# An attention and expert kernel on one core: context statistics spread over 64 tiles, the expert number read a tile ahead, spare rows filled whole, one weight matrix a batch

## The reference

```python
x = x + _L0_xattn(_layernorm(x), ctx, Wq, Wkv, Wo)          # 16 heads of 8, keys from ctx
x = x + _L0_ffn(_layernorm(x), ...)                          # 8 experts, the best one a token, 128->512->128, relu
x = x + _L1_xattn(_layernorm(x), ctx, ...)                   # two attentions of 16 heads of 32: on x (masked), then on ctx
x = x + _L1_ffn(_layernorm(x), ...)                          # 64 experts, the best four a token

def _L0_ffn_ref(x, Wr, br, W1, b1, W2, b2):
    expert_idx = jnp.argmax(xf @ Wr.T + br, axis=-1)
    h = jax.nn.relu(jnp.einsum('td,efd->etf', xf, W1) + b1[:, None, :])
    y = jnp.einsum('etf,edf->etd', h, W2) + b2[:, None, :]
    return y[expert_idx, jnp.arange(xf.shape[0])]

# in the second attention of _L1_xattn the context is normalised first:
yn = _ln(ctx, lny_g, lny_b)      # (ctx - mean) * (var + eps)^-0.5 * g + b
```

## Time and profile before

| | us |
|---|---|
| median of 3 runs | 2547.68 (2545.48 to 2555.09) |
| the profiled execution | 2546.86 |
| its span | 2545.1 |
| TensorE busy | 2252.1 (88%) |
| VectorE busy | 1950.9 (77%) |
| ScalarE busy | 1633.4 (64%) |
| GpSimd busy | 1534.1 (60%) |

### The profile page before, as it was taken

One profiled execution on the slowest core, in us unless ns is written; L12 is line 12 of the kernel. 1 busy time (PEld: TensorE's weight loads), 2 busy tenths in 40 slices (PEclk: granted clock), 3 DMA queues, 4 the chain that ended last, 5 costly groups with the idle time before them and its releaser, 6 DMA issues. The chain is left out here.

```text
span 2545.1 us, 87868 instructions
## 1 busy us (share of the span) xinstructions
PE 2252.1 (88%) x31528; PEld 1772.2 (70%) x31528; DVE 1950.9 (77%) x6038; ACT 1633.4 (64%) x3410; POOL 1534.1 (60%) x2510
## 2 busy tenths in 40 slices
PE   6999899958878999999999999999999999984755
PEld 5777677737876777777777777777777777763543
DVE  4778788756665788888888888888888888864558
ACT  4656566524544778888787787778788777763210
POOL 1555455543543577777677776776767777654456
PEclk9999999979988999999999999999999999995675
DMA  6333432112210011000000000000000000001247
GB/s 146 94 72 78 61 80 74 44 31 59 55 36 6 5 49 62 32 11 10 8 8 7 7 5 7 6 6 6 6 6 5 6 7 5 4 2 25 59 134 240
DMA packets 147867, 99.61 MB, mean 39 GB/s; under 512 B 47690, under 2 KB 129646, under 8 KB 147054
## 3 DMA queue, kind: packets, MB, share of 16 engines
q1 hardware_dynamic: 130798, 78.24, 12.4%
q0 software_dynamic: 16640, 15.76, 2.1%
HBM read 51.59 MB, written 56.80 MB: 43 GB/s over the span
## 5 line engine op out<-in xcount | busy, mean ns | idle before, releaser
L1267 POOL DMA_INDIRECT xs_d<-xpay,dest x256 | 267.4, 1045 | 138.5 <-issue 133.7
L1688 DVE TENSOR_REDUCE rdx<-core 128x16 f32<-128x1920 f32 (+1 forms) x128 | 282.8, 2209 | 54.3 <-PE core L806 54.2
L1169 POOL TENSOR_SCALAR st_h<-st_h 128x1 f32<-128x1 f32 x192 | 43.9, 229 | 354.7 <-DVE st_h L1366 354.5
L1107 ACT ACTIVATE kbd<-core 128x1024 f32<-128x1024 f32 (+1 forms) x256 | 245.8, 1011 | 8.4 <-PE core L844 8.4
L839 PE MATMUL core<-qT,pTm 32*128 32x128 f32 (+1 forms) x4096 | 194.9, 306 | 0.4 <-ACT nm3T L1093 0.4
L806 PEld LDWEIGHTS core<-pTm,qT 32*128 32x128 f32 x4096 | 125.9, 186 | 97.8 <-ACT qT L1111 93.2
L877 PE MATMUL bank<-li,shared 128*128 128x128 f32 x1024 | 147.2, 288 | 34.6 <-ACT shared L1129 34.4
L839 PEld LDWEIGHTS core<-qT,pTm 32*128 32x128 f32 (+1 forms) x4096 | 162.1, 186 | 19.2 <-issue 10.5
L1129 ACT ACT_TABLE_LOAD x128 | 164.2, 1283 | 2.2
L792 PE MATMUL bank<-yT,wk 128*128 128x128 f32 (+1 forms) x1024 | 146.4, 285 | 19.4 <-DVE denT L1627 17.1
L877 PEld LDWEIGHTS bank<-li,shared 128*128 128x128 f32 x1024 | 125.6, 193 | 50.4 <-ACT shared L1129 46.3
(11 more groups left out here) (243 smaller groups left out, 6986.0 us busy)
## 6 DMA issues: line engine op xcount, KB each, us to landing
c_d<-zeros SPq DMA_DIRECT2D x64, 256.0 KB
big<-c_d SPq DMA_DIRECT2D x64, 256.0 KB
big<-in_w SPq DMA_DIRECT2D x3, 2048.0 KB, 8.7
qT<-xs_d SPq DMA_DIRECT2D x72, 64.0 KB
vS<-xs_d SPq DMA_DIRECT2D x64, 65.0 KB, 1.9
xs_d<-zeros SPq DMA_DIRECT2D x8, 512.0 KB
yb<-y_d SPq DMA_DIRECT2D x64, 64.0 KB, 1.8
xs_d<-xpay,dest POOLq DMA_INDIRECT x256, 2.2
```

The lines of the kernel that those rows point to most:

```text
L1107: af(pTb[0:u.T, 2 * k:2 * k + 2, :], core[0:u.T, 2 * k:2 * k + 2, :], ACT.Exp, scale=SCALE).then_inc(s_pexp, 1)
L1267: g_.indirect_dma_start(out=xs1_d, out_offset=bass.IndirectOffsetOnAxis(ap=dest[:, v.bs, k:k + 1], axis=0), in_=xpay[:, v.bs, k, :], in_of ...
L1688: v_.tensor_reduce(nm_part[0], core[:, :, 0:4 * T].rearrange("p g (c t) -> p g c t", c=4), AX.X, ALU.max, negate=True)
```

## The change

- SyncE's order in the attention stage: one matrix a batch at batches 6 to 19, vectors at 20 and 22, eight fills at successive batches 24 to 31, the experts' weights two batches earlier. A fill now writes whole rows of 130 words from `pad_row` (128 zeros and the payload of an empty row), and `start_pads1` is gone.
- The zeroing of the tails (`zero_tail`) is done by SyncE for experts 0 to 3 and by ScalarE for 4 to 7.
- `context_stats` takes one batch a tile on tiles 0 to 63; `context_roots` takes eight batches at a time, after the scatters of tiles 7, 15, ..., 63; the rows are normalised on GpSimd for even batches (`context_even`, from tile 8 on) and on VectorE for odd ones (`context_odd`, from tile 13 on).
- VectorE loads the expert number of tile j+1 right behind `hidden0` of tile j.
- New waits: TensorE for GpSimd's last row (`s_cp`), VectorE for the fills before it uses their source again.

The diff, without the declarations and a few lines that only rename:

```diff
@@ -148,6 +148,7 @@
         ssa = woT0
         ssb = zeros
         xp = sb("xp", [P, 2, P])
+        pad_row = xp.rearrange("p u d -> p (u d)")[:, 0:P + 2]
         z3 = sb("z3", [P, P])
         z3T = sb("z3T", [P, P])
         xnS = sb("xnS", [P, 2, P])
@@ -391,6 +393,13 @@
             for j in range(n):
                 step(j // RING, j % RING, j < n - 1)
             after(n // RING - 1)
+
+        def zero_tail(eng, e):
+
+            at = eng.value_load(filled_i[0:1, e:e + 1], min_val=0, max_val=E0 * REGION0)
+            n = 9 if e == E0 - 1 else 1
+            eng.dma_start(xs_d[bass.ds(at, n * P), :].rearrange("(p a) d -> p a d", a=n),
+                          zeros[:, :].unsqueeze(1).to_broadcast([P, n, P])).then_inc(s_pad, 16)
 
         def earlier(i, k, d):
 
@@ -424,11 +433,14 @@
                 sp.dma_start(xres[:, FIRST:NB, :], x_v[:, FIRST:NB, :]).then_inc(s_x[1], 16)
                 sp.dma_start(ctx_sb[:, FIRST:NB, :], c_v[:, FIRST:NB, :]).then_inc(s_x[1], 16)
 
-            def load_matrices(a):
-                for n, dst in (("wq", wq), ("wk", wk), ("wv", wv), ("li1", li1), ("li2", li2),
-                               ("li3", li3), ("b2c", b2c)):
-                    rows = LAT if (a == 1 and n in ("wk", "wv")) else P
-                    sp.dma_start(dst[a][0:rows, :], t[f"{n}{a}"]).then_inc(s_load, 16)
+            matrices = [(n, dst, a) for a in range(2)
+                        for n, dst in (("wq", wq), ("wk", wk), ("wv", wv), ("li1", li1), ("li2", li2),
+                                       ("li3", li3), ("b2c", b2c))]
+
+            def load_matrix(k):
+                n, dst, a = matrices[k]
+                rows = LAT if (a == 1 and n in ("wk", "wv")) else P
+                sp.dma_start(dst[a][0:rows, :], t[f"{n}{a}"]).then_inc(s_load, 16)
 
             def load_vectors(a):
                 for n, dst in (("li1b", li1b), ("li3b", li3b), ("g_ln", g_ln), ("b_ln", b_ln)):
@@ -451,14 +463,10 @@
 
             def start_rows1(k):
 
-                e = slice(8 * k, 8 * k + 8)
-                sp.dma_start(xs1_v[:, e, 0:P], zeros[:, :].unsqueeze(1).to_broadcast([P, 8, P]))\
+                if k == 0:
+                    sp.wait_ge(s_made, 3)
+                sp.dma_start(xs1_v[:, 8 * k:8 * k + 8, :], pad_row.unsqueeze(1).to_broadcast([P, 8, P + 2]))\
                     .then_inc(s_init1, 16)
-
-            def start_pads1():
-
-                sp.dma_start(xs1_v[:, :, P:P + 2],
-                             padlist1[:, :].bitcast(F32).rearrange("p (e c) -> p e c", c=2)).then_inc(s_init1, 16)
 
             def load_experts0(k):
 
@@ -485,26 +493,21 @@
                     sp.nop(nofuse=True)
                 if u:
                     sp.dma_start(c_rows[u.batch], zeros4).then_inc(s_c0, 16)
-                if u and u.batch in (10, 14):
-                    load_matrices((u.batch - 10) // 4)
-                if u and u.batch in (12, 16):
-                    load_vectors((u.batch - 12) // 4)
-                if u and 18 <= u.batch < 34 and u.batch % 2 == 0:
-                    start_rows1((u.batch - 18) // 2)
-                if u and u.batch == 34:
-                    start_pads1()
-                if u and 36 <= u.batch <= 52 and u.batch % 2 == 0:
-                    load_experts0((u.batch - 36) // 2)
+                if u and 6 <= u.batch < 20:
+                    load_matrix(u.batch - 6)
+                if u and u.batch in (20, 22):
+                    load_vectors((u.batch - 20) // 2)
+                if u and 24 <= u.batch < 32:
+                    start_rows1(u.batch - 24)
+                if u and 34 <= u.batch <= 50 and u.batch % 2 == 0:
+                    load_experts0((u.batch - 34) // 2)
 
             pipeline_a(sp, half_a)
 
 
             sp.wait_ge(s_filled, 1)
-            for e in range(E0):
-                at = sp.value_load(filled_i[0:1, e:e + 1], min_val=0, max_val=E0 * REGION0)
-                n = 9 if e == E0 - 1 else 1
-                sp.dma_start(xs_d[bass.ds(at, n * P), :].rearrange("(p a) d -> p a d", a=n),
-                             zeros[:, :].unsqueeze(1).to_broadcast([P, n, P])).then_inc(s_pad, 16)
+            for e in range(E0 // 2):
+                zero_tail(sp, e)
             for s in range(2):
                 sp.wait_ge(s_sc[s], 32 * (NB // 2))
             sp.wait_ge(s_map, 1)
@@ -866,6 +869,7 @@
                 if h:
                     if h.a:
                         pe.wait_ge(s_c, 1)
+                        pe.wait_ge(s_cp, 1)
                     pe.wait_ge(s_z, h.n(1, 1))
                     last = tr(m0[:, 0:P], zS[:, :], ident)
                     if h.a:
@@ -1059,6 +1063,9 @@
                 if i * RING + k + 2 < TILES0:
                     weights0(i * RING + k + 2)
 
+            act.wait_ge(s_filled, 1)
+            for e in range(E0 // 2, E0):
+                zero_tail(act, e)
             act.wait_ge(s_map, 1)
             act.wait_ge(s_ffnw, 288)
             weights0(0)
@@ -1221,29 +1228,42 @@
                     bounds_check=dst.shape[0] - 1, oob_is_err=False)\
                     .then_inc(s_ysc[k], 16)
 
-            def context_roots():
-
-                pool.wait_ge(s_cvar, 1)
+            def context_roots(k):
+
+                eight = slice(8 * k, 8 * k + 8)
+                pool.wait_ge(s_cvar, k + 1)
                 pool.nop(nofuse=True)
-                g_.tensor_scalar(crs[:, :], cstat[:, :, 1], 1.0, EPS, ALU.mult, ALU.add).then_inc(s_cadd, 1)
-                pool.wait_ge(s_cadd, 1)
+                g_.tensor_scalar(crs[:, eight], cstat[:, eight, 1], 1.0, EPS, ALU.mult, ALU.add)\
+                    .then_inc(s_cadd, 1)
+                pool.wait_ge(s_cadd, k + 1)
                 pool.nop(nofuse=True)
-                g_.tensor_tensor(crs[:, :], crs[:, :], neghalf[0:CTX, :].to_broadcast([CTX, NB]), ALU.pow)\
+                g_.tensor_tensor(crs[:, eight], crs[:, eight], neghalf[0:CTX, :].to_broadcast([CTX, 8]), ALU.pow)\
                     .then_inc(s_crstd, 1)
+
+            def context_even(b):
+
+                pool.wait_ge(s_crstd, b // 8 + 1)
+                pool.nop(nofuse=True)
+                made = g_.tensor_scalar(ctx_sb[:, b, :], ctx_sb[:, b, :], cstat[:, b, 0:1], crs[:, b:b + 1],
+                                        ALU.subtract, ALU.mult)
+                if b == NB - 2:
+                    made.then_inc(s_cp, 1)
 
             def ids_there(j):
                 pool.wait_ge(s_ids[j % RING], j // RING * 32 + 32)
 
             tile_rows = lambda j: ids[:, j:j + 1]
             for j in range(TILES0):
-                if j == NB // 2 + 4:
-                    context_roots()
                 ids_there(j)
                 scatter(Unit(0, 0, RING, j), j % RING, y0_d, tile_rows(j), yS)
+                if j < NB and j % 8 == 7:
+                    context_roots(j // 8)
+                elif j >= 8 and j % 2 == 0:
+                    context_even(j - 8)
 
 
             pool.wait_ge(s_c0, 16 * (CROWS // (4 * P)))
-            pool.wait_ge(s_init1, 16 * 9)
+            pool.wait_ge(s_init1, 16 * 8)
 
 
             def mask_pair(u, k):
@@ -1373,11 +1393,13 @@
             v_.memset(onesb[:, :], 1.0)
             v_.memset(count1[:, :], 0.0)
             v_.memset(nma, 0.0)
+            v_.memset(pad_row[:, 0:P], 0.0)
             v_.memset(v_all[:, :], 0.0).then_inc(s_made, 1)
             dve.wait_ge(s_const, 80)
             copy(count0[:, :], slot0)
             copy(pickb[:, :, :], rS[:, :].rearrange("p (c t) -> p c t", c=4))
             copy(identb[:, :], ident)
+            copy(pad_row.bitcast(I32)[:, P:P + 2], padlist1[:, 0:2])
             copy(ltri[:, :], xx[:, :]).then_inc(s_made, 1)
             for s in range(2):
                 copy(pay_i[:, s, :, 0], cst_i[:, 258 + 4 * s:262 + 4 * s])
@@ -1514,6 +1536,7 @@
 
 
             dve.wait_ge(s_load, 16 * N_LOADS)
+            dve.wait_ge(s_init1, 16 * 8)
             for a in range(2):
                 v_.tensor_tensor(li3b[a][:, :], li3b[a][:, :], li1b[a][:, :], ALU.subtract)
 
@@ -1547,49 +1570,50 @@
 
             def context_stats(b):
 
-                six = (st_c, st_x) if b % 4 else (st_3, st_h)
-                for k in range(2):
-                    v_.bn_stats(six[k][0:CTX, 0:6], ctx_sb[:, b + k, :])
+                six = (st_c, st_x)[b % 2]
+                v_.bn_stats(six[0:CTX, 0:6], ctx_sb[:, b, :])
                 after()
-                for k in range(2):
-                    last = v_.bn_aggr(cstat[:, b + k, :], six[k][0:CTX, 0:6])
-                if b == NB - 2:
-                    last.then_inc(s_cvar, 1)
-
-            def context_rows(b):
-
-                if b == 0:
-                    dve.wait_ge(s_crstd, 1)
-                for k in range(2):
-                    last = v_.tensor_scalar(ctx_sb[:, b + k, :], ctx_sb[:, b + k, :], cstat[:, b + k, 0:1],
-                                            crs[:, b + k:b + k + 1], ALU.subtract, ALU.mult)
-                if b == NB - 2:
```

(41 more changed lines are left out.)

1 line of the change is left out of this document (added).

## The result

| us | before | after |
|---|---|---|
| median (runs) | 2547.00 (2541.42 to 2557.59, 7) | 2514.78 (2510.73 to 2529.78, 7) |
| profiled execution, its span | 2546.86, 2545.1 | 2510.73, 2509.0 |
| TensorE busy | 2252.1 | 2222.0 |
| GpSimd busy | 1534.1 | 1566.8 |

The forecast was 2509, and both medians lie in its range of 2497 to 2530. How it comes together is less tidy than the total.

The account below looks back on a forecast made before the run. It took attention-stage stalls, the handover wait, then VectorE and GpSimd's power (TensorE from tile 45) to bound the kernel; 13.5 + 5.0 + (12.8 - 1.5) + (9.4 - 1.0) = 38.2 us gave 2509, range 2497 to 2530.

Parts of the forecast that it names:

- Term 1: Attention stage: SyncE's reordered loads and whole-row fills remove two long batches, 5.8 and 7.7 us, together 13.5 us.
- third rival: Attention stage: stalls come from where instruction blocks fall, and fall elsewhere; 2522 us in all, chance 0.13.
- second stall: Attention stage, batch of 15.34 us: TensorE idle 4.27 us, read as an instruction block behind the 8-byte packets; 7.7 us.
- first stall: Attention stage, batch of 13.38 us: TensorE's stall, placed after the burst of seven matrices around 121 us; 5.8 us.
- Term 2: Handover to the first experts: tail-zeroing DMAs split between SyncE and ScalarE, at 1.43 us a step; 5.0 us saved.
- Term 3: First expert stage: statistics one batch a tile, expert number loaded early; 12.8 us saved less 1.5 for ties on odd tiles.
- first rival: First expert stage: VectorE stays the bound, its queue stopping at the load wherever it stands; 2522 us, chance 0.10.
- Term 4: First expert stage, GpSimd: 64-column root cut into eight of 8 columns; 9.4 us freed less 1.0, so 8.4.
- fourth rival: GpSimd: the power of eight columns costs nearly what 64 do; slower, 2580 us, chance 0.04.
- the tie: First expert stage: eight tiles take GpSimd 15.3 us against TensorE's 15.2; 1 us charged for a later last scatter.
- second rival: First expert stage: GpSimd becomes the bound, eight tiles taking 16.9 us; 2521 us in all, chance 0.11.
- A later stage changed by more than 5 us: Stages after the first experts: each expected as long as before; such a change was named as showing the prediction wrong.

Follow-up runs that it names:

- sync_only: The kernel before with only SyncE's attention-stage loads changed (one matrix a batch, whole-row fills, no 8-byte DMA); ratio to before 0.9954 (0.9926 to 0.9982).
- after_again: The changed kernel, unchanged, measured and traced a second time; 2508.92 us (6 runs), ratio to before 0.9844 (0.9814 to 0.9874).
- expert_stage_only: The kernel before with only the first expert stage changed (early expert-number load; statistics, roots and rows spread); 2531.16 us, ratio 0.9937 (0.9901 to 0.9973).
- tails_split: The kernel before with only the zeroing DMAs of the tails of experts 4 to 7 moved to ScalarE; one run, 2533.50 us.
- load_ahead: The kernel before with only VectorE's load of tile j+1's expert number moved right behind tile j's prob add; ratio 0.9948 (0.9924 to 0.9972).

## Why the prediction was right, and where it was not

Term 1, SyncE's loads, 13.5 us: the one whose reason failed. The step "removed: 5.8 and 7.7" took two long batches of one trace as what the change takes away, and that nothing comes in their place. The two went, but others of 9 to 12 us stand in every trace of the new loads, on VectorE and ScalarE too. Some of them aren't new: VectorE's idle time at batch 57 is at the same instruction in three traces of the old loads (2.0 to 2.5 us) and in five with whole-row fills (2.5 to 3.9 us). The seven traces with the old loads have an attention stage of 499.9 us on average, the four with the new 500.7: by trace the term is 0 with an uncertainty of a few us, which is the third rival's place (13 per cent). By time it isn't 0: sync_only gives 11.7 (5 to 19), and after_again against expert_stage_only, on the same chip, 22.2, of which the tails have 5.2, so 17, with some 7 either way. Of these 17 the two traces show 3.3 in the attention stage and 7.8 in the 64 experts' stage. 13.5 fits the times in size, but for no reason that the prediction gave; the term's size stays open between 0 (by trace) and 17 (by time).

Its reading of the second stall, an instruction block behind the 8-byte packets, was half of it. TensorE does stop at the edge of a block, and the edge follows the packets; but the scatter that the packets hold up for 14 to 18 us makes the batch long too, and in tails_split without any such stall of TensorE. The first stall's reading, the burst of seven matrices, isn't borne out as a rule: tails_split has the burst and 8.8 us.

Term 2, tails, 5.0: measured 4.4 in the trace and 4.0 alone. The mechanism was right, the step of 1.43 us wasn't: it averages in the one slow issue of 2.64 us, which stays. The last four issues start at 565.76, 566.84, 567.93 and 569.02, each 1.09 us after the one before; 4 x 1.09 = 4.4 us is what the split took away.

Term 3, statistics and load, 11.3: from tile 0 to 40, 654.50 - 577.92 = 76.6 us against 89.4, 12.8 saved, the number forecast without the 1.5 us of ties. The first rival, that the queue stops at the load wherever it stands, fell by load_ahead. The trace of the change and load_ahead agree: TENSOR_LOAD right behind the add is hidden by it.

Term 4, roots, 8.4: tiles 40 to 45 take 663.98 - 654.50 = 9.48 us against 18.87, 9.4 saved. The power of 8 columns at 1.67 kills the fourth rival. The context row was 0.1 us dearer than taken, and the scatters' median grew from 982 to 1064 ns. So GpSimd is nearer to its limit than the sum had it, yet tiles 45 to 71 take 49.84 us against 49.50 before: the tie cost 0.3, not 2.5 us. The second rival is out.

The Trainium skill (SBUF — State Buffer, SBUF: two separate sides) has a GpSimd instruction and a VectorE one in a two-port mode, or with two inputs in SBUF, lock each other out of a shared port for a whole instruction. Beside such a VectorE instruction (0.28 to 0.69 us here) a context row would by that rule last up to its length more than 0.5 us; the longest of 32 took 0.667, the median 0.598. So this trace doesn't show it at its full price. Whether the 8% longer scatter has to do with it isn't known.

What the forecast didn't have is the 64 experts' stage: 125.0 and 129.8 us before, 111.2 and 118.1 after. "A later stage changed by more than 5 us" was named as what would show the prediction wrong, and it came. It goes with TensorE's clock level there: over the stage the mean granted clock was 0.62 where it took 129.8 us, 0.69 at 125.0, 0.79 at 118.1, 0.91 at 111.2 and 0.94 at 110.8, and in all 14 traces the stage is the shorter the higher the clock. The nine traces of kernels that keep some part of before have 117.1 to 129.8 (mean 123.6), the three with the whole change and no filler 111.2 to 118.1 (mean 114.2). Why the end of the program is helped by edits in the first 30% of it isn't known. For the stage itself chance isn't excluded; for the whole execution the clock does differ: 0.945 to 0.954 in the six runs of after_again, 0.930 to 0.946 in the eight of expert_stage_only.

Two smaller signs failed as well: TensorE stood 1.59 us for "issue" at 481 us, and its clock was at the half level from 291 to 295.

So the total hit for a mixed reason, and in part by luck. The firm terms, 2 to 4, give 21.9 + 4.4 = 26.3 us where 24.7 were forecast. The other 6 to 13 (of the 32.1 and 39.7 by the two ratios) that the times show go with stalls and clock levels that differ between executions, where 13.5 had been put down to two particular batches.

On the rule of instruction fetching (the Trainium skill, Runtime: NRT & Kernel Launch, Instruction fetch mechanics: mostly hidden): here the idle times with no engine as their releaser were 1 to 9 us on TensorE, 2 to 4 on VectorE and up to 6.2 on ScalarE. For TensorE the block edges and the move with the packets bear it out that it waited for instructions; in the kernel before, the last packet of instructions had started 5.5 us before the stall ended, so what was late in it isn't seen. For VectorE and ScalarE it is argued only, from the name "remote".

## What to carry to other kernels

Before a stall in a trace is priced, look whether a second trace of the same kernel has it at the same length; a long batch that goes often leaves others longer, and only timed runs of that edit alone can size it. In an engine's queue put a register load right behind a long instruction, a tile before its value is needed; then small work can be spread over more tiles for nothing. A power whose cost grows with the columns can be cut up for a small fee (eight pieces of 1.67 us are 13.4 us instead of 10.6), so that no other work stands behind a long one. Before a mean step is priced, look whether one slow issue is in it.
